# A graph attention layer's gather: one per pair of edge tiles, weighed on ScalarE into a ring of items

## The reference

```python
def _gat(x, ei_src, ei_dst, W, a_src, a_dst, b, heads, out_ch, concat):
    h = (x @ W).reshape(n, heads, out_ch)
    al_s = jnp.einsum('nhc,hc->nh', h, a_src)
    al_d = jnp.einsum('nhc,hc->nh', h, a_dst)
    e = jax.nn.leaky_relu(al_s[src] + al_d[dst], 0.2)
    emax = jax.ops.segment_max(e, dst, num_segments=n)
    ee = jnp.exp(e - emax[dst])
    denom = jax.ops.segment_sum(ee, dst, num_segments=n)
    alpha = ee / (denom[dst] + 1e-16)
    out = jax.ops.segment_sum(h[src] * alpha[:, :, None], dst, num_segments=n)
```

## Time and profile before

| What | Value |
|---|---|
| median of 3 runs | 5002.93 us (4993.8 to 5009.67) |
| the profiled execution | 4995.22 us |
| its span, first to last instruction | 4993.4 us |
| TensorE busy | 3650.3 us (73%) |
| VectorE busy | 2791.1 us (56%) |
| ScalarE busy | 2014.9 us (40%) |
| GpSimd busy | 2025.0 us (41%) |
| layer 3's stage | 3592 to 4323 us of the span, 731 us |

### The profile page before, as it was taken

How to read it: one execution, slowest core, us unless ns; L and a number is a source line. 1 busy time by engine, 2 the same in 40 slices (tenths; PEclk the granted TensorE clock), 3 DMA queues, 4 the chain that set the end, 5 groups by cost and what they waited for, 6 DMA issues and landing times. The chain is left out here.

```text
span 4993.4 us, 76396 instructions
## 1 busy us (share of the span) xinstructions
PE 3650.3 (73%) x19614; PEld 2884.8 (58%) x19615; DVE 2791.1 (56%) x8633; ACT 2014.9 (40%) x6637; POOL 2025.0 (41%) x2092
## 2 busy tenths in 40 slices
PE   5677777695999467778768678776736666667995
PEld 3455554585888346566555566655624444456885
DVE  4477777645122457777666677765735555763112
ACT  0466666421222136667733567666310100121221
POOL 0566666000222025666611466663166666102221
PEclk9778878896999779999988799998857676878998
DMA  2566666253778756776633677665344443204556
GB/s 77 177 176 188 183 185 183 86 150 97 266 258 278 244 211 213 213 226 202 180 121 130 210 214 242 208 179 148 112 153 144 144 127 100 86 31 154 186 182 222
DMA packets 353522, 859.19 MB, mean 172 GB/s; under 512 B 52390, under 2 KB 162829, under 8 KB 344589
## 3 DMA queue, kind: packets, MB, share of 16 engines
q0 software_dynamic: 144384, 455.22, 30.4%
q1 hardware_dynamic: 208780, 399.80, 24.2%
HBM read 770.02 MB, written 84.81 MB: 171 GB/s over the span
## 5 line engine op out<-in xcount | busy, mean ns | idle before, releaser
L1853 POOL DMA_INDIRECT h<-h_table,src_of x944 | 907.6, 961 | 1045.7 <-PE ps L1887 498.6
L1867 PE MATMUL ps<-h,gat_layer_hot 128*128 128x261 f32 (+1 forms) x3136 | 892.2, 435 | 310.9 <-DVE h L2102 90.0
L1867 PEld LDWEIGHTS ps<-h,gat_layer_hot 128*128 128x128 f32 x3136 | 636.5, 213 | 484.7 <-issue 275.6
L734 POOL DMA_INDIRECT edges_rows<-kv_table,src_of x464 | 458.4, 988 | 405.5 <-DVE edges_out_rows L833 150.9
L2125 DVE TENSOR_TENSOR acc<-acc,ps 128x522 f32 (+1 forms) x696 | 417.7, 600 | 305.1 <-PE ps L1867 187.6
L1952 ACT ACTIVATE h<-h,gat_shared 128x128 f32<-128x128 f32 x1872 | 580.7, 389 | 3.7 <-issue 2.7
L1853 POOL DMA_INDIRECT x<-h_table,src_of x448 | 430.7, 961 | 228.0 <-issue 110.5
L1867 PE MATMUL ps<-x,gat_layer_hot 128*128 128x261 f32 (+1 forms) x1504 | 420.8, 428 | 107.3 <-DVE x L2102 37.8
L1021 ACT ACTIVATE acc<-ps,moe_experts_b 128x256 f32<-128x256 f32 (+1 forms) x512 | 200.7, 443 | 614.8 <-PE ps L971 589.7
L1867 PEld LDWEIGHTS ps<-x,gat_layer_hot 128*128 128x128 f32 x1504 | 299.2, 209 | 189.7 <-issue 84.4
L971 PE MATMUL ps<-moe_experts_turned,moe_experts_w 128*128 128x256 f32 (+1 forms) x2048 | 405.7, 357 | 1.9 <-DMA moe_experts_w<-in_L_ffn_W 1.9
(11 more groups left out here) (377 smaller groups left out, 5702.6 us busy)
## 6 DMA issues: line engine op xcount, KB each, us to landing
moe_experts_w<-in_L_ffn_W SPq DMA_DIRECT2D x128, 1024.0 KB
gat_layer_hots<-hot_table SPq DMA_DIRECT2D x174, 562.0 KB
hot_table<-acc SPq DMA_DIRECT2D x58, 562.0 KB
h<-h_table,src_of POOLq DMA_INDIRECT x944
edges_dst_row<-dst_rows SPq DMA_DIRECT2D x58, 256.0 KB
acc<-src_rows SPq DMA_DIRECT2D x58, 256.0 KB
acc<-dst_rows SPq DMA_DIRECT2D x58, 256.0 KB
h_table<-h SPq DMA_DIRECT2D x10, 1280.0 KB
```

The source lines that it names most:

```text
L734: nc.gpsimd.indirect_dma_start(rows[:, r, s, :], None, k.kv_table, bass.IndirectOffsetOnAxis(ap=k.src_of[:, 2 * t + s:2 * t + s + 1], axis ...
L1853: nc.gpsimd.indirect_dma_start(g.rows(t, e, 0, W), None, g.table, bass.IndirectOffsetOnAxis(ap=k.src_of[:, 2 * t + e:2 * t + e + 1], axis= ...
L1867: mm = nc.tensor.matmul(k.ps[t % S * PIECES + p][:, 0:PIECE], hot[:, t % HOTS, e, :], g.rows(t, e, p * PIECE, (p + 1) * PIECE), start=(e = ...
```

## The change

It touches `phase_items`, the class `Gat` and `phase_gat_layer`.

- Layer 3 gathers each pair once, 416 indirect DMAs in place of 464, into a ring of 16 pairs (PAIR_RING) in `h`, with the sources by pair in the new table `src_pair`.
- The ring of items in layer 3 is only the 12 places in `x`. ACT multiplies the pair's rows by the item's weights and writes them there, two 128x256 multiplications for each item. Which place of the pair ring it reads is a register's value, loaded from the new table `item_pair`.
- SP counts the pairs that have landed (`arrived`) and, from the new table `pair_end` and ACT's `scaled`, those whose last item has been multiplied (`freed`). ACT waits on `arrived`, POOL on `freed`.
- The loads of one-hot blocks in layer 3 are issued by ACT instead of SP: four at the start, then one before every second choice.
- DVE in layer 3 no longer multiplies, and PE no longer waits for it.
- HOTS, the ring of one-hots, has 8 places in place of 12, in all three layers.
- `phase_items` makes the three tables, with 5 matmuls and some small DVE operations.

```diff
+PAIR_RING = 16
@@
             dve.wait_ge(made, 3)
+            c.mark(v.tensor_copy(k.item_pair[0:1, :], pair_of[0:1, :]))
+            c(v.tensor_copy(within[0:TILES - 1, :], k.ps[0][0:TILES - 1, 0:1]))
+            c(v.tensor_scalar(reached[0:TILES - 1, :], iota_k[0:TILES - 1, 0:PAIRS], within[0:TILES - 1, 0:1], None, ALU.is_ge))
@@
+        self.pairs = None
+        if heads == 1:
+            self.rings = self.rings[1:]
+            self.pairs = k.h[:].rearrange("p t w -> p (t w)")[:, 0:PAIR_RING * 2 * self.W].rearrange("p (r s w) -> p r s w", s=2, w=self.W)
@@
-    HOTS, NB = 12, 4
+    HOTS, NB = 8, 4
@@
-    by_dve = 1
+    by_dve = 0 if g.pairs is not None else 1
@@
+        def load_hots(eng, b):
+            if b >= NB:
+                eng.wait_ge(masked, 2 * (b - NB) + 2)
+            eng.dma_start(hots[:, b % NB, :], k.hot_table[b]).then_inc(hots_in[b % NB], 16)
+
         @block.sync
         def _(sp):
-            for b in range(ITEMS // 4):
-                if b >= NB:
-                    sp.wait_ge(masked, 2 * (b - NB) + 2)
-                sp.dma_start(hots[:, b % NB, :], k.hot_table[b]).then_inc(hots_in[b % NB], 16)
+            if g.pairs is None:
+                for b in range(ITEMS // 4):
+                    load_hots(sp, b)
+                return
+            for p in range(PAIRS):
+                sp.wait_ge(gathered[p % PAIR_RING], (p // PAIR_RING + 1) * 32)
+                sp.sem_inc(arrived, 1)
+                d = p - PAIR_RING // 2
+                if d >= 0:
+                    items = sp.value_load(k.pair_end[0:1, d:d + 1], min_val=1, max_val=ITEMS)
+                    sp.wait_ge(scaled, items)
+                    sp.sem_inc(freed, 1)
 
         @block.gpsimd
         def _(pool):
+            if g.pairs is not None:
+                for p in range(PAIRS):
+                    if p < PAIR_RING:
+                        pool.wait_ge(made, min(2 * p + 2, CH // 2 - 4))
+                    else:
+                        pool.wait_ge(freed, p - PAIR_RING + 1)
+                    for e in range(2):
+                        nc.gpsimd.indirect_dma_start(g.pairs[:, p % PAIR_RING, e, :], None, g.table,
+                                                     bass.IndirectOffsetOnAxis(ap=k.src_pair[:, 2 * p + e:2 * p + e + 1], axis=0)
+                                                     ).then_inc(gathered[p % PAIR_RING], 16)
+                return
@@
                 pe.wait_ge(marked, t + 1)
-                pe.wait_ge(weighed, t + 1)
+                if by_dve:
+                    pe.wait_ge(weighed, t + 1)
@@
                 last = act.copy(g.rows(t, slice(None), W, FULL), sums(t))
+                if g.pairs is not None:
+                    p = act.value_load(k.item_pair[0:1, t:t + 1], min_val=0, max_val=PAIRS - 1)
+                    act.wait_ge(arrived, p + 1)
+                    for e in range(2):
+                        last = act.mul(g.rows(t, e, 0, D), g.pairs[:, bass.ds(p % PAIR_RING, 1), e, :].rearrange("p a w -> p (a w)"),
+                                       sums(t)[:, e, 0:1])
+                    last.then_inc(scaled, 1)
+                    return
@@
+                    if g.pairs is not None and q % 2 == 0 and NB <= q // 2 + 1 < ITEMS // 4:
+                        load_hots(act, q // 2 + 1)
                     choose(q)
@@
                 last.then_inc(marked, 1)
+                if not by_dve:
+                    return
                 dve.wait_ge(gathered[t % RING], (t // RING + 1) * 32)
```

More of the change, by code:

```diff
@@ L173, in __init__ @@
         self.item_tile = sb("item_tile", [1, ITEMS + 8], I32)
+        self.item_pair = sb("item_pair", [1, ITEMS], I32)
+        self.pair_end = sb("pair_end", [1, PAIRS], I32)
+        self.src_pair = sb("src_pair", [P, 2 * PAIRS], I32)
         self.src_of = sb("src_of", [P, SUBP], I32)
@@ L285, in phase_items @@
         passed = ph.sb("passed", [P, 2, TILES - 1])
-        turn = ph.sb("turn", [P, 1])
+        turn, within = ph.sb("turn", [P, 1]), ph.sb("within", [P, 1])
+        reached, end_f = ph.sb("reached", [P, PAIRS]), ph.sb("end_f", [P, PAIRS])
         iota_k = ph.sb("iota_k", [P, ITEMS])
@@ L361, in _ @@
             mm.then_inc(made, 1)
+            pe.wait_ge(fed, 5)
+            nc.tensor.matmul(k.ps[2][:, 0:PAIRS], k.ones[0:TILES - 1, :], reached[0:TILES - 1, :], start=True, stop=True)
+            for s in range(2):
+                for b in range(2):
+                    mm = nc.tensor.matmul(k.ps[3][:, (2 * s + b) * P:(2 * s + b) * P + GB], src[0:GB, b, s * P:(s + 1) * P],
+                                          k.ident[0:GB, 0:GB], start=True, stop=True)
+            mm.then_inc(made, 1)
         @block.vector
@@ L399, in _ @@
                 c(v.tensor_copy(src_f[:, s:SUBS:2], k.ps[6 + s][:, 0:ITEMS]))
-            dve.sem_inc(fed, 1)
+            dve.sem_inc(fed, 2)
             c(v.tensor_copy(k.src_of[:], src_f[:]))
@@ L415, in _ @@
             dve.sem_inc(rows_out, 1)
+            dve.wait_ge(made, 5)
+            for s in range(2):
+                for b in range(2):
+                    v.tensor_copy(k.src_pair[:, 2 * GB * b + s:2 * GB * (b + 1):2], k.ps[3][:, (2 * s + b) * P:(2 * s + b) * P + GB])
+            c(v.tensor_tensor(end_f[:], k.ps[2][:, 0:PAIRS], iota_k[:, 0:PAIRS], ALU.add))
+            v.tensor_scalar(k.pair_end[0:1, :], end_f[0:1, :], 1.0, None, ALU.add)
 class Moments:
@@ L1814, in phase_gat_layer @@
         hots_in = [ph.sem(f"hots_in{b}") for b in range(NB)]
-        gathered = [ph.sem(f"gathered{r}") for r in range(RING)]
+        gathered = [ph.sem(f"gathered{r}") for r in range(PAIR_RING if g.pairs is not None else RING)]
+        arrived, freed = ph.sem("arrived"), ph.sem("freed")
         cut, chosen, made, masked, picks, dst_taken, cut_link = (
@@ L1958, in softmax @@
                     if c >= 2:
-                        act.wait_ge(weighed, (c - 1) * CH)
+                        act.wait_ge(weighed if by_dve else scaled, (c - 1) * CH)
                     act.activation(g.sums[:, c % 2, :, 0:H], back.rearrange("p h s -> p s h"), ACT.Exp).then_inc(exped, 1)
@@ L1963, in softmax @@
                     act.activation(old[:], old[:], ACT.Exp).then_inc(old_exped, 1)
+            if g.pairs is not None:
+                for b in range(NB):
+                    load_hots(act, b)
             act.wait_ge(cut, 1)
@@ L2086, in _ @@
                     v.memset(rows[:, :, :, FULL:g.pitch], 0.0).then_inc(padded, 1)
-                dve.wait_ge(padded, 2)
+                dve.wait_ge(padded, len(g.rings))
             def weigh(t):
```

## The result

The changed kernel takes 5035.2 us in the median of eight runs (5022.2 to 5041.3), the kernel before 5004.4 beside it: a ratio of 1.0068, 95% interval 1.0058 to 1.0078. Forecast was 4945, and a range up to 5015. **It is slower by 31 us where 58 were to be gained**, and the time is, to the microsecond, that of rival C.

The account below looks back on a forecast made before the run. Layer 3 was taken as bound by the consumers of gathers, TensorE waiting for VectorE. Terms 27 + 31 + 11 - 10 - 1 = 58 us gained, 5002.9 to 4945 us; forecast band 4920 to 4975 (55%), 8-in-10 range 4885 to 5015.

Parts of the forecast that it names:

- rival C: Layer 3: ScalarE becomes the engine waited for; ten uncovered pauses cost 100 us against 69 gained: 5035 us; chance 10%.
- the first part: Layer 3's bound: POOL itself waits for places, so the consumers end last; among these TensorE waits for VectorE.
- VectorE's relief: Layer 3: VectorE loses the weighing, gaining 27 us in the maximum stretches and 31 us in the scoring stretches.
- The tail: Layer 3's end after the last chunk's weights: gathers now end last, 68 us in place of 79, gain 11 us.
- POOL, 48 gathers fewer: Layer 3: 60 us less POOL work, used in the tail, worth nothing before it because POOL waits.
- ScalarE's queue: Layer 3: weighing takes ScalarE 0.9 us an item; four items with choices need 7.8 us against 10.6, so it fits: 0.
- ScalarE's pauses: Layer 3: more records make ten pauses in place of four, mostly hidden by a three-item lead: 10 us lost, ends 0 and 100.
- The table loads: Layer 3: 58 issues of one-hot loads moved from SP's queue to ScalarE's, inside its slack: 0.
- Relay, HOTS, `phase_items`: SP's relay time hidden, 0; eight one-hot places in place of 12, 0; short VectorE operations in `phase_items`, 1 us lost.
- Scoring stretches: Sign in layer 3, where items are summed while the next chunk's scores are made: near 2.65 us an item.
- the wait for L2159: Sign in layer 3: TensorE's waits for VectorE's one-hots, forecast under the earlier line number L2095, below 30 us.
- D: Rival, layer 3: the gathers do bound it, so 48 fewer save 60 us: 4943 us; sign, ScalarE waiting for `arrived`; chance 8%.

Follow-up runs that it names:

- e6: Kernel before, POOL's wait in layer 3 rounded up to the next twelve summed items, so gathers come in rows of 24: 5124.7 us to 5002.6, ratio 1.0233.
- e5: Kernel after, with one more POOL wait: a gather also waits for TensorE's sums of the pair 16 places back, less four items; ratio 0.9993 to before.
- e1: Kernel before with only the weighing in layer 3 moved to ScalarE, gathers still one per half item: ratio 0.9987 to the kernel before.
- e12: e1 with a memset on POOL and a wait for it behind every gather: ratio 1.0001 to the kernel before.
- e2: Kernel after without register addresses and SP's relay; ring places known at build, some items read a neighbouring pair's rows: ratio 1.0026 to before.
- e4: e2 with the loads of the one-hot tables back on SP's queue: ratio 1.0035 to the kernel before.
- e13: e5 with 24 places for pairs in place of 16: ratio 1.0012 to the kernel before.
- e8: Kernel before with a 128x64 memset on POOL and a wait for it after every gather of layer 3, spacing them: ratio 0.9979 to before.
- e7: e4 with the wait of e5: ratio 0.9957 to the kernel before.
- e3: e2 with SP's relay and its register loads kept; only ScalarE's address is known at build: ratio 1.0046 to the kernel before.
- e9: e6 with each gather of layer 3 bringing 64 columns of a row in place of 256: ratio 1.0241 to the kernel before.
- e15: e6 with each gather of layer 3 bringing 32 rows in place of 128: ratio 1.0295 to the kernel before.
- e10: Kernel after with the memset and wait of e8 behind every gather, 1.39 us apart in place of 1.25: ratio 1.0047 to the kernel before.
- e16: e8 with the memset behind the gathers of items 0 to 191 alone: ratio 1.0021 to the kernel before.
- e18: e14 with POOL held to one item's lead in place of four, on a fifth chip: 4444.5 us, ratio 1.0011 to the kernel before.
- e17: e6 with each gather of layer 3 replaced by two POOL memsets, on a fifth chip: ratio 0.9832 to the kernel before.
- e14: Kernel after with e5's wait, e8's memset behind every gather and 24 places for pairs: ratio 0.9962 to the kernel before.

## Why the prediction was wrong, step by step

The step that failed stands in the first part: POOL waits, "so the gathers are not what ends last". That is true of its semaphores, and it led to steps in which a gather off the path costs nothing to anyone, and VectorE's busy time is what TensorE waits for. The runs showed that issuing gathers in a row stops the engines that are on the path: 122 us lost in e6, which changes nothing but when POOL may go on, and 37 won back in e5 by one wait. VectorE's relief, put at 58 us, is worth 6 (e1) or 0 (e12).

1. **VectorE's relief, 58 us.** The waits for L2095 and L2102 in the earlier trace rows were real, but VectorE comes to these lines behind L1998, and there, by the same trace, it stood 143.8 us in 41 places for TensorE's products, which reached it 4.9 us late in the median (e6). With POOL still, four items take 6.4 us, and there VectorE is full (10.37 of 10.4 us, e6). In the maximum stretches the kernel after did gain 46 us, but with 23 gathers in the first of them in place of 47: VectorE's relief and fewer gathers are mixed there, and no run parts them. In the scoring stretches the 31 us turned into 95 lost.
2. **The tail, 11 us gained, gather-bound.** The last weights come at 4276.45, the layer ends 87.6 us later and not 68. Behind the weights POOL issues 46 gathers, near the 50 forecast, but it is busy only 30.3 of the last 65.9 us: not back to back, so not the bound. What else holds the tail no run isolates.
3. **POOL, 48 gathers fewer, worth nothing.** The term that was missing is here: places given free by ScalarE, when it runs ahead, let POOL issue rows of 10 to 16 (28 in e2 and e4) where scores are still made. Whether fewer gathers are worth anything by themselves no run isolates. The unforeseen gain of 37 us at the start fits the same cause: 32 gathers fill the ring, where before POOL ran on to 3696 and ScalarE's first pause stands at the end of that row. With a ring of 24 the start is 22 us longer (e13 to e5, on different chips).
4. **ScalarE's queue, 0.9 us an item.** Right: its copies stand 0.9 us apart when it is free, two multiplications take 0.91.
5. **ScalarE's pauses, 10 us, from 0 to 100.** The number of records does lengthen them: counted as rows of steps of 0.7 us and its multiples they are 136 us in the kernel after and some 30 in e2. But they are not all that the time hangs on: in e5, 37 us faster, they are still some 130, and in e8, where they are below 10, the late word from TensorE stays. With the relay they cost some 21 us (after to e2) or 18 (e5 to e7), twice my value and far from C's 100.
6. **The table loads, 0.** Right (e4).
7. **Relay, HOTS, `phase_items`, 1 us.** The relay's 4 to 10 us (e3 to e2) aren't clear of noise; the others can't be seen.

Of the signs: the maximum stretches at 2.2 to 2.7 us an item (2.6 said), 416 gathers and ScalarE 280 us busy (300 said) came about as said. Scoring stretches are at 3.4 to 3.9 and not 2.65, the wait for L2159 is 104.8 and not below 30. The waits for ScalarE's multiplications, C's sign, are 10.9 us, not over 40, and `arrived` (D's) held ScalarE for some 24: by my own signs neither rival had happened. **C named the time, 5035, by a wrong sum**: some 20 us of what was lost are of its kind, and the 37 to 39 of the rows (e5, e7) were in nobody's list. That its 5035 was met is luck. By the rule of the Trainium skill (Runtime: NRT & Kernel Launch, Instruction fetch mechanics), fetching is mostly hidden and C costs nothing; as far as the pauses go with the number of records, e2 and e7 show it costing 18 to 21 us. That what starts them is a fetch no run shows.

What stays open: by which path POOL's issuing reaches the other engines, TensorE's word to VectorE above all. It is not the bytes (e9), not the number of rows (e15), not ScalarE's multiplications (e1), and a distance of 1.39 us doesn't cure it by itself (e10). POOL's being busy without DMAs was only tried on a chip without the effect. And every run here has a span and a clock recorded by the profiler, so whether the pauses stand without it isn't shown.

## What to carry to other kernels

An engine that others hardly wait for can still cost them time by when it issues: look at what the others do while it issues in an unbroken row, in windows cut at the row's ends, and not at its waits alone. Hold an issuing engine to the pace of the engine that ends last, and not to that of one that can run ahead; here one wait was worth 37 us. Where a wait looks long, find out when the work that it waits for ended by its own record: here that was 5 us earlier in the median and up to 30. And before work is moved off an engine that is "waited for", try the move alone: e1 would have said 6 us in place of 58.

## What the runs showed of the hardware

- On the four chips of e1 to e16, while POOL issued indirect DMAs 1.25 us apart, TensorE, ScalarE, VectorE and SP fell, some 4 to 10 us into the row, to one instruction in 0.7 or 1.4 us, in step with one another, or stood: one matmul and nothing of VectorE in the last 12 us of a row of 24 (e6).
- There VectorE went on 29.8 us after the last record of the products that it waited for, and 0.1 us after them with POOL still (e6). In the kernel before this was 4.9 us in the median, on the fifth chip 0.09 (e18). Whether semaphore or record is off is open.
- A row of 24, 30 us long, held up the items by 27 us where scores are made in e6 (33.5 against 6.4), with a quarter of the bytes by 27 (e9), with a quarter of the rows by 28 (e15). Two such rows lengthened a maximum stretch by only 9 to 13 us.
- A gather of 32 rows took POOL 0.88 us, one of 128 rows 0.95.
- The chip of e17 and e18 showed no such pauses in the layer, and ran the kernel before in 4439.7 us, 11% below the 4999 to 5046 of the four others, with TensorE's clock at 0.887 in e18's mean where e14 has 0.853. Why that chip is without them is open.
- Beside POOL's memsets VectorE's multiplications of 128x256 took 550 ns (e17), beside gathers 360 (before).
